# A transformer block with attention maxima folded into the scores: where the maxima are turned, and how eight PSUM banks are shared

## The chip, the cores and the metric

One NeuronCore of a Trainium2 chip runs the whole kernel. The metric is the device time of one execution in microseconds (us), as the median of several. The engines are PE (TensorE matmul, with its weight loads shown apart as PEld), DVE (VectorE), ACT (ScalarE), POOL (GpSimd) and SP (SyncE, which here only issues DMAs).

## The reference

A block of a diffusion transformer over a batch of 16 sequences of 256 tokens and 512 channels, with 16 heads of 32 channels:

```python
xn = adaln(x, cond, ln1);  q, k, v = split(xn @ qkv_w.T)
x = x + attn(rope(q), rope(k), v) @ sa_out_w.T            # layer 0: self attention
xn = adaln(x, cond, ln2)
q = rope(xn @ q_w.T); k = rope(ctx @ k_w.T); v = ctx @ v_w.T
x = x + attn(q, k, v) @ ca_out_w.T                        # layer 1: cross attention
xn = adaln(x, cond, ln3)
x = x + gelu(xn @ ffn_w1.T + ffn_b1) @ ffn_w2.T + ffn_b2
```

`adaln` normalizes each token and scales and shifts it by vectors made from the condition. All is in float32.

## The kernel before, in words

Two stages follow one another: attention, with both layers interleaved (0 to about 1450 us), and the feed-forward part (from there to the end). The change touches only the attention stage.

**Precision.** Each float32 operand is split in a high part, rounded to the type that TensorE multiplies fast, and a low rest. A product is three matmuls (high by high, high by low, low by high). The loops at lines 505 (k and q) and 501 (v and o) do so for projections; the score product has its parts stacked along the contraction, in 96 rows of `qT` and `kT`.

**Softmax.** Scores are computed twice. "scores" (line 515) puts queries on the partitions, and DVE takes the negated maximum of each row (line 739). "weigh" (line 535) computes the transposed scores with 8 more contraction rows, by which the maxima are subtracted inside the matmul; ACT takes the exponential (line 635), POOL adds the two halves of the keys (line 795), and "mix" (lines 548 and 555) multiplies by the values and sums. For the 8 rows, DVE splits the maxima of 4 heads in two parts ("max_split": a cast on line 747 and a difference on line 749), PE transposes them ("max_turn", line 524), and ACT copies them into `qT` ("max_copy", line 627). The first weigh of those 4 heads waits for the copy.

**Order.** There are 32 items (16 batch entries by two layers), each with 16 heads, that is 512 heads. A group G is 8 heads and has two halves of 4. `stage_order` writes one order of steps, and each engine runs its own steps in just this order. A place is a third of a head: scores of head n stand at place 3n, and weigh of head n - 8 at place 3n + 1. Everything else is put at places with `put`: within item i, with p = 48 i, the steps for item i + 2 (its norm, its turned x, its projections). A step of group G half h stands at 24 G + 12 h plus an offset. At equal places the order is that of the `put` calls.

**PSUM.** There are eight banks: `NS` banks used in turn by scores, weigh and max_turn (`score_users`), `NB` banks used in turn by projections, the turned x and the modulation (`bank_users`), and one for mix. A step waits on PE until the user of its bank NS (or NB) turns earlier has been read: a score by line 739, a weigh by the exponential, a max_turn by its copy; a k or q projection by the two rope products on DVE (lines 714 and 718), v by an ACT copy (line 613), o by a DVE add (line 724), turned x by ACT (line 590).

```python
score_users = [step for step in order if step[0] in ("scores", "weigh", "max_turn")]
def scores_left(step):
    n = score_turn[step] - NS
    ...
    return {"scores": max_done, "weigh": exp_done, "max_turn": maxes_copied}[old[0]], nth[old]
```

**x.** "turn_x" (PE line 488, in two halves) transposes the normalized x, ACT scales it (line 590) and rounds it ("x_high", line 599), POOL forms the rest ("x_low", line 772), and SP loads the next item's x once the second half is turned (line 802).

Of the kernel before, what the change touches and what calls it, by code (L numbers as in the profile page):

```python
# [9 lines left out]
F32R = mybir.dt.float32r  # L10
# [14 lines left out]
def stage_order(B):  # L25

    N = 2 * B
    places = {}

    def put(place, *step):
        places.setdefault(place, []).append(step)

    def weight_rows(place, rows, gap):
        for n, row in enumerate(rows):
            if n < 4:  # L40
                put(place, "w_load", *row)
        for n, row in enumerate(rows):
            put(place + gap * (n + 1), "w_split", *row)
            if n + 4 < len(rows):
                put(place + gap * (n + 1), "w_load", *rows[n + 4])

    def layer_rows(layer, m):
        return [(layer, m, c) for c in range(KC)]

    def spread(first, count, units):  # L50

        last = {}
        for n, unit in enumerate(units):
            place = first + n * count // len(units)
            put(place, *unit)
            last[unit[:4]] = place
        return last

    def project(m, i, t):
        return [("project", m, i, t, c) for c in range(KC)]  # L60

    def turns(last):
        for step, place in last.items():
            put(place + 5, "rope_high", *step[1:])
            put(place + 7, "rope_low", *step[1:])
            put(place + 7, "spill", *step[1:])

    def shares(*stretches):

        last = {}  # L70
        for first, count, units in stretches:
            last.update(spread(first, count, units))
        return last

    for i in range(-1, N):
        p, ahead = 48 * i, i + 2
        if 0 <= i < 2:
            put(p + 24, "mod_load", i + 1, 0)
            put(p + 24, "mod_load", i + 1, 1)
            for c in range(KC):  # L80
                put(p + 44 + c, "mod", i + 1, c)
                if c + 2 < KC:
                    put(p + 44 + c, "mod_load", i + 1, c + 2)
        if ahead < N + 2:
            put(p - 13, "stats", ahead, 0)
            put(p - 5, "stats", ahead, 1)
            put(p - 4, "norm", ahead)
            put(p + 1, "scale", ahead, 0)
            put(p + 5, "scale", ahead, 1)
            x_place = p + (31 if ahead == B else 20)  # L90
            for half in range(2):
                put(x_place + 3 * half, "turn_x", ahead, half)
                put(x_place + 2 + 3 * half, "x_high", ahead, half)
                put(x_place + 4 + 3 * half, "x_low", ahead, half)
        if ahead < N:
            if ahead >= B:
                put(p - 10, "ctx_load", ahead)
                put(p + 6, "ctx_split", ahead)
            k, q, v = (project(m, ahead, 0) + project(m, ahead, 1) for m in "kqv")
            if ahead < B:  # L100
                turns(shares((p + 29, 6, k[:4]), (p + 45, 7, k[4:])))
                spread(p + 66, 11, v)
            else:
                turns(spread(p + 18, 11, k))
                if ahead == B:
                    spread(p + 45, 7, v)
                else:
                    shares((p + 29, 6, v[:4]), (p + 45, 7, v[4:]))
            turns(spread(p + 52, 14, q))
        if i >= 1:  # L110
            put(p + 20, "res_load", i - 1)

            spread(p + 36, 9, [("project", "o", i - 1, t, c) for cs in (range(KC - 1), (KC - 1,)) for t in range(T) for c in cs])
            put(p + 47, "store", i - 1)
        if i == B - 2:
            weight_rows(p + 6, layer_rows(1, "k"), 2)
            weight_rows(p + 30, layer_rows(1, "v"), 2)
            weight_rows(p + 38, layer_rows(1, "q"), 2)
        if i == B:
            weight_rows(p + 45, layer_rows(1, "o"), 2)  # L120
        if i == N - 2:
            weight_rows(p - 14, [("ffn", k % (3 * KC), 0) for k in range(KC, 4 * KC)], 4)
    for G in range(2 * N):
        for half in range(2):
            put(24 * G + 12 * half + 10, "max_split", G, half)
            put(24 * G + 12 * half + 15, "max_turn", G, half)
            put(24 * G + 12 * half + 16, "max_copy", G, half)
        if G:
            put(24 * G - 20, "stack", "k", G)
            put(24 * G - 17, "stack", "q", G)  # L130

    for quad in range(4 * N):
        place = 3 * (4 * quad + LAG + 5) + 2
        for n, kind in enumerate(("mix", "invert", "divide", "o_split", "o_low")):
            put(place + 2 * n, kind, quad)

    rows = {m: layer_rows(0, m) for m in MATS}
    for row in rows["k"]:
        yield ("w_load", *row)
    for c in range(KC):  # L140
        yield ("mod_load", 0, c)
    for t in range(T):
        yield ("stats", 0, t)
    yield ("norm", 0)
    for t in range(T):
        yield ("scale", 0, t)
    for before, after in zip(rows["k"], rows["q"]):
        yield ("w_split", *before)
        yield ("w_load", *after)
    for c in range(KC):  # L150
        yield ("mod", 0, c)
    for half in range(2):
        yield ("turn_x", 0, half)
    for half in range(2):
        yield ("x_high", 0, half)
        yield ("x_low", 0, half)
    for before, after in zip(rows["q"], rows["v"]):
        yield ("w_split", *before)
        yield ("w_load", *after)
    yield from project("k", 0, 0)  # L160
    yield from project("k", 0, 1)
    for before, after in zip(rows["v"], rows["o"]):
        yield ("w_split", *before)
        yield ("w_load", *after)
    for m, after in ("kq", "qv"):
        for t in range(T):
            yield ("rope_high", m, 0, t)
            yield ("rope_low", m, 0, t)
            yield ("spill", m, 0, t)
            if t == 0:  # L170
                yield ("stack", m, 0)
        if m == "k":
            yield ("pick",)
        for t in range(T):
            yield from project(after, 0, t)
    for row in rows["o"]:
        yield ("w_split", *row)
    for place in sorted(place for place in places if place < 0):
        yield from places.pop(place)

    HEADS = 16 * N
    for n in range(HEADS + LAG + 6):
        for part in range(3):
            if part == 0 and n < HEADS:
                yield ("scores", n)
            if part == 1 and n >= LAG and n - LAG < HEADS:
                yield ("weigh", n - LAG)
            for step in places.pop(3 * n + part, ()):
                yield step
    assert not places, places  # L190
    yield ("res_load", N - 1)
    for t in range(T):
        yield from project("o", N - 1, t)
    yield ("store", N - 1)


def block_kernel(nc, x, condT, ctxT, lnT, lnb, attnT, w1T, b1, w2T, b2, cos, sin, pick, ident_in, x1, x2, out):
# [63 lines left out]
        elif (step[0] == "project" and step[4] == 0) or (step[0] == "mod" and step[2] == 0):  # L261
            bank_users.append(step)
    bank_turn = {step: n for n, step in enumerate(bank_users)}
    NB = 4

    score_users = [step for step in order if step[0] in ("scores", "weigh", "max_turn")]
    score_turn = {step: n for n, step in enumerate(score_users)}
    NS = 3

    with ExitStack() as whole:  # L270

# [31 lines left out]
        with ExitStack() as stage:  # L303
# [349 lines left out]
            def attention_vector(eng):  # L653
                eng.memset(neg_half[:, :], -0.5).then_inc(constants_set, 1)
                eng.memset(max_parts[:, :, 0:ROWS], 0.0).then_inc(parts_cleared, 1)
                for step in order:
# [84 lines left out]
                    elif kind == "max_split":  # L741
                        G, half = step[1:]
                        eng.wait_ge(max_done, HG * G + OH * (half + 1))
                        if nth[step] > 1:
                            eng.wait_ge(max_turned, nth[step] - 1)
                        mine = neg_max[G % 2][:, :, OH * half:OH * (half + 1)]
                        eng.tensor_copy(max_parts[:, :, ROWS:ROWS + OH].bitcast(F32R), mine).then_inc(max_hi_done, 1)
                        eng.wait_ge(max_hi_done, nth[step])
                        eng.tensor_tensor(max_parts[:, :, ROWS + OH:MROWS], mine, max_parts[:, :, ROWS:ROWS + OH],
                                          ALU.subtract).then_inc(max_split, 1)  # L750
                    elif kind == "divide":
                        quad = step[1]
                        eng.wait_ge(den_inverted, quad + 1)
                        eng.tensor_tensor(o_sb[:, :], ps_o[:, 0, 0:L], o_sb[:, :], ALU.mult).then_inc(o_divided, 1)
# [459 lines left out]
```

## Time and profile before

| | us |
|---|---|
| median of 3 runs | 2187.68 (2186.64 to 2192.2) |
| the profiled execution | 2184.93 |
| its span in the trace | 2183.1 |
| PE busy in the span | 2051.2 (94%) |
| DVE, ACT, POOL busy | 1111.4, 1029.1, 860.9 |
| mean granted clock of TensorE, as a share of full speed | 0.978 |

A row of a group of instructions gives line, engine, operation, output and inputs with shapes, count, busy time, mean ns of one, and how long the engine sat idle before them with the releaser. A row of the chain of waits gives who waited for whom, us in total, number of times, longest. A row of the timeline gives start, duration, engine, line, operation, count, and in brackets the idle time before it. Matmuls are pipelined and their ends are modelled: two rows that follow each other without a gap overlap by some 0.16 us.

### The profile page before, as it was taken

To read this page: it belongs to the slowest core of one execution; us is meant where nothing else is said; L and a number is where in the kernel's file an instruction comes from. 1 tells how busy PE (TensorE), PEld (TensorE's weight loads), DVE (VectorE), ACT (ScalarE), POOL (GpSimd) and SP (SyncE) were. 2 spreads that over 40 slices of the span, in tenths; PEclk is the share of its full clock that TensorE was granted. 3 is DMA by queue.
4 is the path that set the end of the run, shared out by engine and by line. 5 is a ranking of instruction groups with operands and counts; after the bars stand their busy time and mean duration, and the time that the engine had idled before them with its cause. 6 is when DMAs were issued, how large, how long until landed. Compare 5 with 4: busy or idle time off the path is not lost. (4 is left out here: it accounts for less than half of the span.)

```text
span 2183.1 us, 37400 instructions
## 1 busy us (share of the span) xinstructions
PE 2051.2 (94%) x13632; PEld 1687.3 (77%) x13632; DVE 1111.4 (51%) x1940; ACT 1029.1 (47%) x1858; POOL 860.9 (39%) x946
## 2 busy tenths in 40 slices
PE   6799999999998899999999998789999999999999
PEld 6688777777777678878878887568888888888887
DVE  4554766766676667767666666633222221222221
ACT  2344555555555656656656655644232332323322
POOL 1344555555555566666666665530101100011010
PEclk9888999999999999999999999899999999999999
DMA  5655656656556677576676676631101101011010
GB/s 180 178 154 145 174 160 168 166 155 174 160 156 173 174 198 204 160 208 175 170 198 179 175 202 172 153 121 48 58 20 39 58 1 58 20 39 58 1 39 20
DMA packets 239346, 277.93 MB, mean 127 GB/s; under 512 B 13888, under 2 KB 194368, under 8 KB 239168
## 3 DMA queue, kind: packets, MB, share of 16 engines
q1 hardware_dynamic: 239168, 275.55, 45.5%
q8 instruction: 112, 1.84, 0.4%
q14 instruction: 66, 0.54, 0.1%
HBM read 183.23 MB, written 92.27 MB: 126 GB/s over the span
## 5 line engine op out<-in xcount | busy, mean ns | idle before, releaser
L795 POOL TENSOR_TENSOR sums_sb<-prob 128x256 f32<-128x256 f32 x512 | 381.0, 749 | 392.9 <-ACT prob L635 391.1
L739 DVE TENSOR_REDUCE neg_max<-ps_s 128x2 f32<-128x512 f32 x512 | 346.4, 686 | 363.0 <-PE ps_s L515 360.7
L635 ACT ACTIVATE prob<-ps_s 128x512 f32<-128x512 f32 x512 | 305.7, 597 | 464.4 <-PE ps_s L535 462.0
L1093 DVE TENSOR_TENSOR h_lo<-h_sb,h_hi 128x512 fp32r<-128x512 f32 x128 | 92.2, 721 | 515.2 <-ACT h_hi L1054 515.2
L1050 ACT ACTIVATE h_sb<-ps_h,b_sb 128x512 f32<-128x512 f32 x128 | 88.1, 688 | 490.7 <-PE ps_h L993 490.7
L789 POOL TENSOR_TENSOR rope_c<-rope_c,rope_s 128x512 f32<-128x512 f32 x128 | 175.6, 1372 | 143.3 <-DVE rope_s L718 142.2
L515 PE MATMUL ps_s<-kT,qT 96*128 96x256 f32 x1024 | 224.1, 300 | 8.0 <-DVE neg_max L739 5.7
L535 PE MATMUL ps_s<-qT,kT 104*128 104x256 f32 x1024 | 221.0, 298 | 7.8 <-DVE neg_max L739 6.1
L515 PEld LDWEIGHTS ps_s<-kT,qT 96*128 96x128 f32 x1024 | 167.3, 192 | 72.7 <-issue 52.1
L505 PE MATMUL ps_g<-xx_hi,w_hi 128*128 128x256 f32 x1024 | 213.1, 290 | 5.5 <-POOL xx_lo L772 3.1
L505 PE MATMUL ps_g<-xx_hi,w_lo 128*128 128x256 f32 x1024 | 210.0, 287 | 0.0
L505 PE MATMUL ps_g<-xx_lo,w_hi 128*128 128x256 f32 x1024 | 209.6, 287 | 0.0
L1107 POOL TENSOR_TENSOR f_res<-f_res,b_sb 128x512 f32<-128x512 f32 x32 | 44.1, 1407 | 389.8 <-DMA f_res<-x_after_cross 389.8
L535 PEld LDWEIGHTS ps_s<-qT,kT 104*128 104x128 f32 x1024 | 170.9, 194 | 25.5 <-DVE neg_max L739 8.4
L505 PEld LDWEIGHTS ps_g<-xx_hi,w_hi 128*128 128x128 f32 x1024 | 163.3, 195 | 7.0 <-POOL xx_lo L772 3.5
L505 PEld LDWEIGHTS ps_g<-xx_lo,w_hi 128*128 128x128 f32 x1024 | 162.6, 195 | 0.0
L505 PEld LDWEIGHTS ps_g<-xx_hi,w_lo 128*128 128x128 f32 x1024 | 162.0, 194 | 0.0
L548 PE MATMUL ps_o<-prob,v_sb 128*32 128x256 f32 x2048 | 141.1, 394 | 2.5 <-ACT prob L635 2.5
L627 ACT ACTIVATE qT<-ps_s 8x1024 fp32r<-8x1024 f32 x128 | 130.3, 1018 | 3.1
L524 PE MATMUL ps_s<-ident,max_parts 128*104 128x128 f32 x256 | 54.8, 297 | 75.5 <-DVE neg_max L739 70.0
L772 POOL TENSOR_TENSOR xx_lo<-xT,xx_hi 128x512 fp32r<-128x512 f32 x68 | 101.5, 1493 | 31.6 <-ACT xx_hi L599 31.6
L731 DVE TENSOR_TENSOR rot_lo<-rope_c,rot_hi 128x512 fp32r<-128x512 f32 x128 | 107.1, 837 | 8.3 <-ACT rot_hi L620 8.1
(114 smaller groups left out, 4453.1 us busy)
## 6 DMA issues: line engine op xcount, KB each, us to landing
kT<-k_turned SPq DMA_DIRECT2D x192, 256.0 KB, 5.3
qT<-q_turned SPq DMA_DIRECT2D x64, 512.0 KB, 6.9
k_turned<-rot_hi SPq DMA_DIRECT2D x64, 256.0 KB, 4.6
k_turned<-rot_lo SPq DMA_DIRECT2D x64, 256.0 KB, 4.6
q_turned<-rot_hi SPq DMA_DIRECT2D x64, 256.0 KB, 2.4
q_turned<-rot_lo SPq DMA_DIRECT2D x64, 256.0 KB, 2.5
qT<-q_turned SPq DMA_DIRECT2D x64, 256.0 KB, 7.8
xn<-in_x SPq DMA_DIRECT2D x16, 512.0 KB, 4.9
```

What stands on the lines that cost most here:

```text
L505: ins = eng.matmul(ps_g[:, b, s * L:(s + 1) * L], w[:, row, (T * s + t) * P:(T * s + t + 1) * P], a[:, c, :], start=c == 0 and j == 0 and ...
L515: ins = eng.matmul(ps_s[:, score_bank(step), t * L:(t + 1) * L], qT[0:ROWS, G % NG, j, t * P:(t + 1) * P], kT[0:ROWS, G % NG, j, :], start ...
L535: ins = eng.matmul(ps_s[:, score_bank(step), t * L:(t + 1) * L], kT[:, G % NG, j, t * P:(t + 1) * P], qT[:, G % NG, j, :], start=True, sto ...
L548: ins = eng.matmul(ps_o[j * HD:(j + 1) * HD, 0, 0:L], v_sb[i % NV][:, k, c * P + j * HD:c * P + (j + 1) * HD], prob[:, (OH * quad + j) % N ...
L627: eng.activation(qT[ROWS:MROWS, G % NG, OH * half:OH * (half + 1), :], ps_s[ROWS:MROWS, score_bank(step), 0:L].unsqueeze(1).broadcast_to([ ...
L635: eng.activation(prob[:, n % NP, :, :].rearrange("p t l -> p (t l)"), ps_s[:, score_bank(step), :], ACT.Exp, scale=HD ** -0.5).then_inc(ex ...
L731: eng.tensor_tensor(rot_lo[:, n % NT, :, :], rope_c[n % 2][:, :, :], rot_hi[:, n % NT, :, :].bitcast(F32), ALU.subtract).then_inc(rot_lo_d ...
L739: eng.tensor_reduce(neg_max[G % 2][:, :, j], ps_s[:, score_bank(step), :].rearrange("p (t l) -> p t l", l=L), AX.X, ALU.max, negate=True). ...
L772: eng.tensor_tensor(lo[:, ks, :], xT[:, ks, :], hi[:, ks, :].bitcast(F32), ALU.subtract).then_inc(x_low_done, 1)
L789: eng.tensor_tensor(rope_c[n % 2][:, :, :], rope_c[n % 2][:, :, :], rope_s[:, :, :], ALU.add).then_inc(rope_added, 1)
L795: eng.tensor_tensor(sums_sb[:, n % NP, :], prob[:, n % NP, 0, :], prob[:, n % NP, 1, :], ALU.add).then_inc(halves_added, 1)
L1093: eng.tensor_tensor(h_lo[a % NH][:, :], h_sb[a % 2][:, :], h_hi[a % NH][:, :].bitcast(F32), ALU.subtract).then_inc(h_lo_done, 1)
```

## The change

The transposition of the maxima is put four places later, and the copy with it. The turned x of an item is put four places earlier (16 instead of 20; the item that begins layer 1 keeps its 31), so that its first half comes ahead of the values' projection of the item before. Scores get four banks and projections three. The cast of the maxima to the rounded type is written as a maximum over an axis of one element, with the same input and output.

```diff
-            x_place = p + (31 if ahead == B else 20)
+            x_place = p + (31 if ahead == B else 16)
...
             put(24 * G + 12 * half + 10, "max_split", G, half)
-            put(24 * G + 12 * half + 15, "max_turn", G, half)
-            put(24 * G + 12 * half + 16, "max_copy", G, half)
+            put(24 * G + 12 * half + 19, "max_turn", G, half)
+            put(24 * G + 12 * half + 20, "max_copy", G, half)
...
-    NB = 4
+    NB = 3
...
-    NS = 3
+    NS = 4
...
-                        eng.tensor_copy(max_parts[:, :, ROWS:ROWS + OH].bitcast(F32R), mine).then_inc(max_hi_done, 1)
+                        eng.tensor_reduce(max_parts[:, :, ROWS:ROWS + OH].bitcast(F32R), mine.unsqueeze(3), AX.X,
+                                          ALU.max).then_inc(max_hi_done, 1)
```

## Rows read from the trace of the kernel before

**Rows 1.** The page: PE over the span; then busy us by engine, 800 to 1340.

```profile
PE 2051.2 (94%) x13632; PEld 1687.3 (77%) x13632; DVE 1111.4 (51%) x1940; ACT 1029.1 (47%) x1858; POOL 860.9 (39%) x946
...
800.00:1340.00 540.00, 522.79 (x4269) 434.67 (x4268) 371.98 (x661) 334.04 (x623) 356.76 (x388) 1.00 0.68 185
```

**Rows 2.** Chain of waits, PE and its weight loads, 80 to 680 us.

```profile
PE ps_s L524 <- DVE neg_max L739: 33.7, 27, 1.5
...
PEld ps_s L524 <- DVE neg_max L739: 46.0, 38, 1.7
```

**Rows 3.** Chain of waits, PE, 680 to 800 us.

```profile
PE ps_s L524 <- DVE neg_max L739: 11.8, 5, 5.4
PE ps_s L535 <- DVE neg_max L739: 3.8, 2, 3.1
```

**Rows 4.** Chain of waits, PE and its weight loads, 800 to 1340 us.

```profile
PE ps_s L524 <- DVE neg_max L739: 17.2, 26, 1.2
...
PEld ps_s L524 <- DVE neg_max L739: 24.9, 40, 1.4
```

**Rows 5.** Chain of waits, PE, 1340 to 1470 us.

```profile
PE ps_s L524 <- DVE neg_max L739: 7.3, 5, 3.6
PE ps_s L515 <- DVE neg_max L739: 4.8, 1, 4.8
```

**Rows 6.** Timeline of PE: a max_turn that waited, and one that did not.

```profile
439.26 0.40 PE L515 MATMUL ps_s<-kT,qT 96*128 96x256 f32 x2
441.15 0.43 PE L524 MATMUL ps_s<-ident,max_parts 128*104 128x128 f32 x2 [1.50 <-DVE neg_max L739]
...
443.89 0.50 PE L515 MATMUL ps_s<-kT,qT 96*128 96x256 f32 x2
...
451.92 0.39 PE L501 MATMUL ps_g<-w_hi,xx_lo 128*128 128x512 f32 x1
452.15 0.38 PE L524 MATMUL ps_s<-ident,max_parts 128*104 128x128 f32 x2
```

**Rows 7.** Timeline of DVE, then POOL, in the same microseconds.

```profile
438.61 1.21 DVE L747 CAST max_parts<-neg_max 128x8 fp32r<-128x8 f32 x1
439.85 0.64 DVE L749 TENSOR_TENSOR max_parts<-neg_max,max_parts 128x8 f32<-128x8 f32 x1
440.42 1.28 DVE L739 TENSOR_REDUCE neg_max<-ps_s 128x2 f32<-128x512 f32 x2
...
438.50 1.29 POOL L789 TENSOR_TENSOR rope_c<-rope_c,rope_s 128x512 f32<-128x512 f32 x1 [2.17 <-DVE rope_s L718]
```

**Rows 8.** Lines 747 and 749: ns least/median/greatest, first and last start.

```profile
L747 DVE CAST max_parts<-neg_max x128: 154/684/1223, 85.0 to 1432.4; 128x8 fp32r<-128x8 f32 x128
...
L749 DVE TENSOR_TENSOR max_parts<-neg_max,max_parts x128: 166/168/662, 85.2 to 1432.8; 128x8 f32<-128x8 f32 x128
```

**Rows 9.** Timeline in layer 1: end of a q projection, the following weigh, the rope.

```profile
1119.33 0.40 PE L505 MATMUL ps_g<-xx_lo,w_hi 128*128 128x256 f32 x2
...
1122.15 0.40 PE L535 MATMUL ps_s<-qT,kT 104*128 104x256 f32 x2
...
1120.37 0.68 DVE L718 TENSOR_TENSOR rope_s<-ps_g,sin_sb 128x512 f32<-128x512 f32 x1
```

**Rows 10.** The copy (page); timeline of ACT and PE ahead of a half's first weigh.

```profile
L627 ACT ACTIVATE qT<-ps_s 8x1024 fp32r<-8x1024 f32 x128 | 130.3, 1018 | 3.1
...
1135.03 0.62 ACT L620 ACTIVATE rot_hi<-rope_c 128x512 fp32r<-128x512 f32 x1
...
1136.40 0.40 PE L535 MATMUL ps_s<-qT,kT 104*128 104x256 f32 x2
```

**Rows 11.** Start-up: DVE reads the first q projection; a wait of PE.

```profile
48.36 0.68 DVE L718 TENSOR_TENSOR rope_s<-ps_g,sin_sb 128x512 f32<-128x512 f32 x1
...
PE ps_g L488 <- DVE xn L678: 14.1, 1, 14.1
```

**Rows 12.** Timeline of DVE and PE where layer 1 begins.

```profile
728.44 0.69 DVE L663 BATCH_NORM_STATS2 stats<-xn 128x6 f32<-128x512 f32 x1 [3.89 <-DMA xn<-x_after_self]
...
729.78 0.67 PE L524 MATMUL ps_s<-ident,max_parts 128*104 128x128 f32 x2 [5.37 <-DVE neg_max L739]
```

## The prediction

> **What bounds the kernel now.** I read the page of the profile first: PE is busy 94% of the span, and in a steady stretch of layer 1 for 522.79 of 540 us, with DVE at 372, ACT at 334 and POOL at 357 [rows 1]. So PE sets the time, and the only time to be had without fewer matmuls is what PE sits idle. The chain of waits, asked for PE alone in four stretches, says where: nearly all of it stands before line 524, max_turn, and is ended by the maximum on DVE [rows 2 to 5]. The four rows of line 524 make 33.7 + 11.8 + 17.2 + 7.3 = 70.0 us, in 63 waits.
>
> Who is late is seen in one wait. max_turn starts at 441.15, after 1.50 us idle [rows 6]. On DVE the cast and the difference of the maxima are through at 440.49, but PE waits longer, until the first of the two maxima that start at 440.42 ends, at 440.42 + 0.69 = 441.11 [rows 7]. That is the score two heads back: with three banks, max_turn takes the bank of that score. So the wait is one for a bank, behind a DVE queue that the split itself makes long: cast 1.21 and difference 0.64, where the shortest of each are 0.154 and 0.166 us [rows 8]. The cast started 0.11 us after POOL's rope addition (438.50 to 439.79) and ended 0.03 after it [rows 7].
>
> **How large the stall is.** The printed 1.50 understates it, since the end of the matmul before is modelled. From start to start the waiting max_turn comes 1.89 us after its predecessor, and the one that did not wait 0.23 us [rows 6]: the stall is 1.66, 0.16 more than printed. With 0.16 for each printed wait, 80 to 680 us holds 33.7 + 27 x 0.16 = 38.0; the weight loads, which see small stalls too, say 46.0 [rows 2]. I take 42. 800 to 1340 us: 17.2 + 26 x 0.16 = 21.4 against 24.9 [rows 4], I take 23. 680 to 800: 11.8 + 3.8 + 7 x 0.16 = 17 [rows 3]. After 1340: 7.3 + 4.8 + 6 x 0.16 = 13 [rows 5], of which line 524 has 8.
>
> **The change, part by part.**
>
> *max_turn four places later, with four score banks.* In the new order its bank was last used by the score three places after the one that it waits for now, and PE comes to it after one more pair of scores and two weighs. The order around a half is then: score, weigh, projection, mix, score, weigh, max_turn. In the case of rows 6 the new max_turn stands behind the score at 443.89, while both maxima end by 440.42 + 1.28 = 441.70 [rows 7]: 2 us to spare, and 0.5 still if the stall of 1.66 is taken off. The wait could pass to the next step that needs the late maximum. With four banks that is the score now at 443.89. Without the stall (1.66) and the two transposes (0.13) PE comes there at 442.10, 0.99 us after 441.11. So in the steady stretches nothing is late in its place, and the 42 and the 23 go.
>
> *The cast as a maximum.* The trace has no such small maximum in SBUF. Bounds: 0.154 us, the shortest cast [rows 8], and 0.69, a maximum over 512 elements from PSUM [rows 7]. I take 0.17, by the neighbours of the same 8 elements [rows 8]. On the path it is worth nothing once max_turn stands later, as DVE has the margin above; it widens that margin. By how much, the trace bounds: the pair now ends at 440.49 and began at 438.61. If neither instruction is held up, it ends at 438.95; if the difference is held up in the cast's place until POOL's addition ends at 439.79 [rows 7], at 439.96, so the margin of 0.99 grows by 0.5 to 1.5 us. Here a rule speaks against this part. The Trainium skill, SBUF — State Buffer, on the shared port pair, says that DVE in a two-port mode, or with two inputs from SBUF against a GpSimd operation that reads SBUF, locks out GpSimd and is locked out by it. By that rule the new first instruction is free and the old second one is not, so most of the wait moves from line 747 to line 749; the trace agrees so far as line 749 has durations of up to 662 ns. I take the small gain, 0.5.
>
> *The copy four places later.* The copy takes 1.02 us [rows 10] and the first weigh of the half waits for it. It moves behind one more exponential and the two ACT steps that invert a denominator, in layer 1 also behind a rotation's high part in one half of four. There ACT is through at 1135.03 + 0.62 = 1135.65, but instructions overlap by 0.1, so the copy would run from 1135.55 to 1136.57, and the weigh that needs it comes at 1136.40, or 1136.53 with max_turn (0.13) now ahead of it [rows 10]. That leaves a new wait of 0.04 plus the signal: I take 0.15, bounded by 0 and by a whole copy, 1.02. It is one half in four: about 13 items between 800 and 1340, 2 us. In the other halves no rotation stands ahead of the copy, or the weigh comes later, so I cost them at nothing; the cover is 0.5 us or so, and thin.
>
> *Three banks for projections.* The tightest new pairing in steady running is the second half of the turned x, which takes the bank of the second q projection. That ends on PE at 1119.73, its rope is read out by 1120.37 + 0.68 = 1121.05, and the new turn_x stands just behind the weigh that starts at 1122.15, that is at 1122.39 [rows 9]: 1.3 us to spare, some 0.9 when PE arrives a stall earlier and DVE does not quite follow. Cost 0, bounded by one rope's length (1.3 us) in each of 30 items, 40 us. At start-up the second v projection now waits for the first q rope, out at 49.04; that may be a few us, but PE then idles 14.1 us for the normalized x anyway [rows 11], so 0.
>
> *turn_x four places earlier.* It issues the same 8 transposes. On ACT its scaling comes ahead of an exponential of an earlier head; on POOL x_low comes earlier by the same; on SP the next x load is issued about 3.5 us earlier and passes ahead of a q spill, which has more than ten places until it is stacked. Nothing on PE waits for these. 0.
>
> *Where layer 1 begins (680 to 800).* DVE is held there by a DMA (3.89 us before the statistics, then max_turn idle 5.37) [rows 12] and by weight splits. These stay: the item that begins the layer keeps its place. PE now can go on until the score three places later, which in the steady case is 443.89 - 441.15 - 0.13 = 2.6 us of work [rows 6]. So the long waits, 5.37 [rows 12], 3.1 and another that must be about 4 in the rest of the 11.8 [rows 3], shrink by about 2.5 each, or 7.5, and of the 4 us of short ones nearly all goes: 11 of 17.
>
> *The last heads (after 1340).* There are fewer projections between scores, so the copy's margin is gone: the new waits there I put at up to 1 us in each of the last 8 halves, 5 us in all; the old 13 shrink by 10. Net 5, bounded by -5 and 13.
>
> **The sum.** 42 + (23 - 2) + 11 + 5 = 79 us. The profiled execution took 2184.93, so 2106; the median shown is 2.75 above it. Predicted median 2187.7 - 79 = 2109 us, 3.6% less. The bounds of the terms: at the least 38 + (21 - 2) + 6 - 5 = 58, with 6 where layer 1 begins; at the most 46 + 25 + 17 + 13 = 101. That is 2130 and 2087. The upper bounds of the copy (1.02 us in about 30 halves) and of the third bank (40 us) come on top of these and are the first rival's.
>
> **The rivals.**
>
> 1. *The stall goes, but part of it comes back on a thinner margin*: the copy late at more than one half in four, or the turned x at its bank. Each costs 0.5 to 1 us, in 30 to 60 places, 30 us: 2139. For it: margins of 0.04, 0.5 and 0.9 us as worked out above, and that without its stalls PE runs ahead of ACT and DVE. Against: DVE and ACT have a third of their time free [rows 1]. Chance 0.17.
>
> 2. *It comes out slower: the copy is late at every half.* Place: the first weigh of each half, waiting for line 627. Price: 128 halves; it turns the sign when the mean wait exceeds 79/128 = 0.62 us, that is when copies come about 1.2 us later than reckoned, for instance because ACT stands in front of them waiting for a rope sum from POOL. With a mean wait of 0.8: 2109 + 102 = 2211. Against: ACT is busy 334 of 540 us [rows 1], and so has the time to catch up between two halves. Chance 0.05.
>
> 3. *The change does not remove the wait, as another step takes it over at once*, the pair of scores behind it. That would need the maximum 1 us later than in rows 7. Then about a third of each stall goes, by the places gained: 2160 to 2185. The part within 0.3% of now has a chance of 0.03, the rest 0.03.
>
> A change of under 0.3%, some 6 us, could not be told from none here.
>
> **How the numbers follow.** The forecast as worked out has 0.72, and its time is the prediction. Rivals 1 to 3 have 0.17, 0.05 and 0.06. The range goes from 2092, near the most that the terms allow, to 2148, which takes in rival 1; about 0.13 is left above it and 0.05 below. Faster by over 0.3%: 0.72 + 0.17 + 0.03 = 0.92; within: 0.03; slower: 0.05.
>
> **What would show it.** In the profile of the changed kernel PE's wait at line 524 for line 739 should be under 10 us in all instead of 70, with nothing of it between 200 and 660 or 800 and 1340. An item of layer 0 should take some 3 us less (42 us over the 14 items between 80 and 680 us). Line 747 should read about 170 ns throughout, and line 749 a median well above its 168 [rows 8] if it takes over the hold-up. A new row, line 535 waiting for ACT's copy (line 627), should hold 2 to 8 us; if it holds more than 30, rival 1 or 2 is at work. A wait of line 488 for line 718 tells that three banks are too few. A wait of line 515 for line 739 of more than 20 us would be rival 3. The forecast is wrong if PE's idle time falls and the span does not.

## The result, and the profile after

The changed kernel takes 2099.64 us (median of 4 runs, 2094.36 to 2100.82) against 2188.91 us before: a ratio of 0.9586, with a 95% interval of 0.9565 to 0.9608, so 4.1% less. The forecast was 2109, with a range of 2092 to 2148. The profiled execution has a span of 2098.8 us, 84.3 less than before.

The page of the changed kernel, its first line; then the chain of waits of PE over the whole span, the longest first, against [rows 2 to 5]:

```profile
PE 2034.9 (97%) x13632; PEld 1686.8 (80%) x13632; DVE 1076.0 (51%) x1940; ACT 1037.9 (49%) x1858; POOL 864.0 (41%) x946
...
PE ps_g L477 <- DMA prob<-in_lnT: 12.9, 1, 12.9
PE ps_g L488 <- DVE xn L678: 10.4, 1, 10.4
PE ps_s L535 <- ACT qT L627: 9.8, 6, 3.0
PE ps_g L505 <- issue: 5.5, 2, 3.1
PE ps_g L501 <- DVE rope_s L718: 4.5, 2, 2.7
PE ps_s L535 <- DVE neg_max L739: 3.5, 3, 1.4
PE ps_s L515 <- DVE neg_max L739: 2.8, 2, 2.6
```

The 70.0 us of line 524 are gone from the list, all of them. What is left stands at the two ends, and for a few microseconds at the change of layers. The windows of the changed kernel (length, then busy us of PE, PEld, DVE, ACT and POOL with their instructions, the granted clock, the DMA share and GB/s) show a PE that is busy for 459.43 of 460 us in layer 1, where [rows 1] had 522.79 of 540:

```profile
780.00:1240.00 460.00, 459.43 (x3774) 383.53 (x3775) 312.92 (x582) 294.57 (x542) 310.34 (x342) 1.00 0.66 189
80.00:640.00 560.00, 556.90 (x4486) 475.79 (x4486) 376.58 (x691) 327.61 (x599) 323.81 (x367) 0.97 0.64 180
640.00:780.00 140.00, 131.95 (x1047) 109.57 (x1046) 97.60 (x171) 88.92 (x165) 87.72 (x94) 0.98 0.72 203
1240.00:1366.00 126.00, 111.15 (x886) 84.92 (x884) 77.50 (x144) 81.84 (x156) 76.38 (x90) 0.95 0.56 153
```

The timeline of PE at a max_turn of the changed kernel, to be held against [rows 6]. From start to start it follows by 0.23 us, the spacing of the one that did not wait:

```profile
404.60 0.39 PE L501 MATMUL ps_g<-w_hi,o_lo 128*128 128x512 f32 x1
404.83 0.38 PE L524 MATMUL ps_s<-ident,max_parts 128*104 128x128 f32 x2
404.96 0.48 PE L515 MATMUL ps_s<-kT,qT 96*128 96x256 f32 x2
```

The two instructions of the split, against [rows 8] (the new cast is on line 747, the difference now on line 750):

```profile
L747 DVE TENSOR_REDUCE max_parts<-neg_max x128: 143/150/160, 88.3 to 1347.1; 128x8 fp32r<-128x8 f32 x128
...
L750 DVE TENSOR_TENSOR max_parts<-neg_max,max_parts x128: 166/496/1056, 88.5 to 1347.3; 128x8 f32<-128x8 f32 x128
```

The first is never held up, at most 160 ns where the cast went to 1223. The second has taken over: its median went from 168 to 496 ns.

Whom they wait for can be counted in the same traces. In the kernel before, 71 of the 128 casts and 44 of the 128 differences took over 300 ns, and every one of these 115 ended within 0.06 us of the end of an addition on POOL (line 789 or 795). In the changed kernel the same holds for all 73 differences over 300 ns, while 71 of the 128 new first instructions ran wholly inside a POOL instruction and took no longer for it. No run moved POOL's work, so this is a coincidence in time, though one without an exception. By the rule of the Trainium skill (SBUF — State Buffer, the shared port pair) a DVE instruction with two inputs from SBUF is blocked while a GpSimd operation that reads SBUF holds the pair; the trace agrees, with the 73 of 73.

**Where the time came from.** Each item has one small DVE instruction on line 674, in its norm, which stands two items ahead (that of item 18 stands where item 16 begins, the first of layer 1). The differences of its start between two traces say how far ahead a kernel is there, and their differences what each stretch gave. In the kernel before, the stretches end at 107, 679, 782 and 1308 us. The last column but one takes the rest, up to the end of the span. Worked out from the timelines, us gained against the kernel before, rounded so that each row adds up:

| kernel | up to item 3 | 3 to 16 | 16 to 18 (layers change) | 18 to 31 | after 31 | in all |
|---|---|---|---|---|---|---|
| changed | -0.9 | 42.0 | 8.6 | 18.8 | 15.8 | 84.3 |
| a_place | 1.6 | -12.3 | 1.3 | -23.8 | -6.5 | -39.7 |
| a_banks | -0.6 | -7.0 | -2.7 | -9.6 | 5.8 | -14.1 |
| a_cast | -2.0 | 21.0 | -0.2 | 11.6 | 5.2 | 35.6 |
| a_x | -2.5 | 1.8 | -2.4 | -7.3 | 0.7 | -9.7 |
| b_no_place | 0.2 | 24.1 | 0.4 | 17.2 | 8.0 | 49.9 |
| b_no_banks | 1.5 | 14.3 | 0.2 | -0.8 | -4.6 | 10.6 |
| b_no_cast | 2.5 | 41.8 | 10.6 | 19.6 | 12.9 | 87.4 |
| b_no_x | 0.8 | 9.5 | 10.3 | 3.6 | 15.7 | 39.9 |
| c_at17 | 0.6 | 41.6 | 5.2 | 23.6 | 14.2 | 85.2 |
| c_at21 | -0.2 | -4.0 | 7.8 | -7.7 | 0.4 | -3.7 |
| c_ends | 2.3 | 41.9 | 11.5 | 18.8 | 14.9 | 89.4 |
| d_mix | 1.3 | 41.9 | 9.1 | 22.1 | 12.1 | 86.5 |

These come from one execution each. The first column scatters by some 3 us among kernels with the same steps there, so no more should be read from it.

### The profile page after: what moved, and what is told of

It reads as the page before. It is cut to its first block and busy times, and to the rows that moved or that the text cites. A ratio compares the mean times of both kernels' runs of the same rounds, so it can differ in the third digit from the quotient of the medians.

```text
span 2098.8 us, 37400 instructions
## 1 busy us (share of the span) xinstructions
PE 2034.9 (97%) x13632; PEld 1686.8 (80%) x13632; DVE 1076.0 (51%) x1940; ACT 1037.9 (49%) x1858; POOL 864.0 (41%) x946
## 5 line engine op out<-in xcount | busy, mean ns | idle before, releaser
L796 POOL TENSOR_TENSOR sums_sb<-prob 128x256 f32<-128x256 f32 x512 | 403.4, 793 | 337.2 <-ACT prob L635 335.7
L535 PE MATMUL ps_s<-qT,kT 104*128 104x256 f32 x1024 | 210.3, 288 | 14.6 <-ACT qT L627 9.8
L620 ACT ACTIVATE rot_hi<-rope_c 128x512 fp32r<-128x512 f32 x128 | 80.5, 629 | 64.6 <-POOL rope_c L790 59.1
L501 PE MATMUL ps_g<-w_hi,xx_hi 128*128 128x512 f32 x256 | 105.5, 412 | 4.5 <-DVE rope_s L718 4.5
```

What stands on the lines that cost most here:

```text
L501: ins = eng.matmul(ps_g[:, b, :], a[:, c, t * P:(t + 1) * P], w[:, row, :], start=c == 0 and j == 0, stop=c == KC - 1 and j == 2)
L535: ins = eng.matmul(ps_s[:, score_bank(step), t * L:(t + 1) * L], kT[:, G % NG, j, t * P:(t + 1) * P], qT[:, G % NG, j, :], start=True, sto ...
L796: eng.tensor_tensor(sums_sb[:, n % NP, :], prob[:, n % NP, 0, :], prob[:, n % NP, 1, :], ALU.add).then_inc(halves_added, 1)
```

## The experiments

Twelve kernels were run. Medians, and ratios to the kernel before with their 95% intervals:

| kernel | us | ratio |
|---|---|---|
| a_place: the later place alone | 2222.98 | 1.0156 (1.0138 to 1.0173) |
| a_banks: the banks alone | 2197.0 | 1.004 (1.0026 to 1.0054) |
| a_cast: the cast alone | 2150.03 | 0.9826 (0.9809 to 0.9842) |
| a_x: the earlier x alone | 2194.44 | 1.0031 (1.002 to 1.0041) |
| b_no_place: changed, place undone | 2136.77 | 0.976 (0.9744 to 0.9777) |
| b_no_banks: changed, banks undone | 2174.55 | 0.9926 (0.9904 to 0.9949) |
| b_no_cast: changed, cast undone | 2097.9 | 0.9587 (0.9567 to 0.9607) |
| b_no_x: changed, x undone | 2144.39 | 0.9796 (0.978 to 0.9813) |
| c_at17: max_turn at 17 | 2099.91 | 0.96 (0.9585 to 0.9615) |
| c_at21: max_turn at 21 | 2187.32 | 0.9994 (0.9981 to 1.0006) |
| c_ends: three edits at the ends | 2097.78 | 0.9588 (0.9573 to 0.9602) |
| d_mix: 17 in layer 1, 19 elsewhere | 2097.15 | 0.9576 (0.9563 to 0.9589) |

The four parts alone give +35, +9, -38 and +6 us, together +12. All at once they give -89. So no part's worth can be told without the others.

### a_place: the later place alone

```diff
-            put(24 * G + 12 * half + 15, "max_turn", G, half)
-            put(24 * G + 12 * half + 16, "max_copy", G, half)
+            put(24 * G + 12 * half + 19, "max_turn", G, half)
+            put(24 * G + 12 * half + 20, "max_copy", G, half)
```

> The kernel before, with max_turn and its copy four places later and nothing else. Theory (the wait is for a PSUM bank, and both the later place and a fourth score bank are needed): with three banks the weigh that stood behind max_turn now takes the bank of that same score, so the stall of 1.66 us moves from line 524 to line 535 and stays; line 524 waits under 5 us, line 535 for line 739 some 50 to 70; time 2175 to 2190 us. Rival (the later place alone is enough): 2105 to 2130 us, and line 535 waits no more than before.

Measured: 2222.98 us, slower than both forecasts. The chain of waits of PE:

```profile
PE ps_s L535 <- DVE neg_max L739: 52.2, 52, 3.8
PE ps_s L515 <- ACT qT L627: 40.1, 36, 3.5
```

The first row is the theory's: the wait went from line 524 to the weigh behind the old place, at nearly its old size (52.2 us), since with three banks that weigh takes the bank of the very same score. The second row was in neither forecast. With three banks the score pair that comes three turns behind max_turn takes max_turn's own bank, which is free only when ACT has made the copy. At the old place the step three turns behind was a weigh, and in the changed kernel, with four banks, it is the first weigh of the half, which needs the copy anyway. A bank that steps use in turn has two waits to it: the one of the step that takes it, and the one of the step that takes it next.

### a_banks: the banks alone

```diff
-    NB = 4
+    NB = 3
-    NS = 3
+    NS = 4
```

> The kernel before, with four banks for scores and three for projections and nothing else. Theory: max_turn then takes a bank that is long free and waits only for the split itself, which ends 0.6 us ahead of the maximum in the traced case; about 2.1 us go in each item of layer 0 (14) and 1.1 in each of layer 1 (13), some 45 us, less about 4 us at start-up, where a values' projection waits for a rope: 2140 us, 2128 to 2155; the releaser of line 524 becomes line 749. Rival (banks do not matter, the maxima are just late): 2185 to 2195.

Measured: 2197.0 us, so the expected gain of 45 us did not come. The chain of waits of PE:

```profile
PE ps_s L524 <- DVE max_parts L749: 34.9, 34, 4.2
PE ps_s L535 <- DVE neg_max L739: 20.4, 20, 6.3
PE ps_g L505 <- DVE rope_s L718: 14.2, 15, 0.9
PE ps_g L488 <- ACT v_sb L613: 11.2, 14, 0.8
```

The releaser of line 524 is now line 749, the split, as foretold: the bank is no longer what it waits for. But it still waits, for the split, half as long as before (34.9 against 70.0). And the wait for the bank has in part passed on: with four banks the weigh just behind the old place takes the bank of the late score, and line 535 waits 20.4 us where the kernel before had 6.1. On top of both, three projection banks cost 14.2 + 11.2 us that the kernel before had not. I had taken these as free, from an order in which x was already moved.

### a_cast: the cast alone

```diff
-                        eng.tensor_copy(max_parts[:, :, ROWS:ROWS + OH].bitcast(F32R), mine).then_inc(max_hi_done, 1)
+                        eng.tensor_reduce(max_parts[:, :, ROWS:ROWS + OH].bitcast(F32R), mine.unsqueeze(3), AX.X,
+                                          ALU.max).then_inc(max_hi_done, 1)
```

> The kernel before, with the cast of the maxima as a maximum over one element and nothing else. Theory: the first instruction of the pair is never held up (150 us x 128 in the changed kernel's trace read 150 ns each), but line 750 takes over the hold-up, so the maximum behind it comes only 0.5 us earlier, in some 50 stalls: 25 us, 2165 (2155 to 2180). Rival A (neither is held up once the cast is gone): each stall shrinks by up to 1.5 us, 2110 to 2135. Rival B (nothing): 2189.

Measured: 2150.03 us, 38 less, just beyond the theory's 2155 and far from either rival. The wait of PE, and the two instructions:

```profile
PE ps_s L524 <- DVE neg_max L739: 35.5, 50, 3.8
...
L747 DVE TENSOR_REDUCE max_parts<-neg_max x128: 141/151/161, 87.0 to 1397.0; 128x8 fp32r<-128x8 f32 x128
...
L750 DVE TENSOR_TENSOR max_parts<-neg_max,max_parts x128: 166/498/1029, 87.2 to 1397.1; 128x8 f32<-128x8 f32 x128
```

The wait halved, 70.0 to 35.5. On average the first instruction of the pair went from 618 to 151 ns and the second from 333 to 521: 0.47 us saved, 0.19 us taken back. What is left, 0.28 us, makes 36 us over 128 pairs, near the 38 measured. In the stretches the gain is 1.6 us for an item of layer 0 (21.0 / 13), where there are two long stalls and one short.

### a_x: the earlier x alone

```diff
-            x_place = p + (31 if ahead == B else 20)
+            x_place = p + (31 if ahead == B else 16)
```

> The kernel before, with x turned four places earlier and nothing else. Theory: nothing on PE waits for it, no change within 6 us of the kernel before (2183 to 2195). Rival: the DMA at the layer's start or POOL's order shifts the stalls, a loss or gain of over 10 us.

Measured: 2194.44 us, a ratio of 1.0031: a small loss, at the edge of the expected band. In the table it stands in layer 1 (-7.3), and in the chain of waits of PE at the old stall, which has 79 waits instead of 63:

```profile
PE ps_s L524 <- DVE neg_max L739: 76.2, 79, 4.2
```

Why the maxima come later with x turned earlier was not looked into. Nothing was gained by this part where there are four banks for projections.

### b_no_place, b_no_banks, b_no_cast, b_no_x: the change without one part

Each is the changed kernel with the hunk of its part turned back, as in the four diffs above with plus and minus exchanged.

> The changed kernel with max_turn and its copy at their old place. Theory: four banks let max_turn wait for the split alone, and the split is 0.5 us earlier by the new cast, so only 0.3 to 0.6 us stay of the stalls of 1.66 in layer 0 and about 0.1 in layer 1; the late copies of the last heads go too: 2105 to 2120. Rival (the place carries the gain): 2150 or more.

Measured: 2136.77 us, between the two. The split is waited for again, and the late score's bank too. The rows of PE over the span, then of the weight loads from 100 to 680 us:

```profile
PE ps_s L524 <- DVE max_parts L750: 19.5, 23, 4.5
PE ps_s L535 <- DVE neg_max L739: 9.0, 8, 5.1
...
PEld ps_s L524 <- ACT prob L635: 11.0, 15, 3.8
PEld ps_s L535 <- DVE neg_max L739: 10.1, 28, 1.0
```

The later place is worth 37 us, in layer 0 above all (24.1 against 42.0). There the weight loads show two small waits of about the same sum: at line 524, in the same number as PE's waits for the split, and at the weigh behind it, which takes the bank of the late score. The forecast took the stalls that stay at 0.6 us and less; they are 0.85 on average (19.5 / 23), 1.0 with the 0.16.

> The changed kernel with three score banks and four for projections. Theory: the stall stands at line 535 behind the same maximum, shorter by 0.5 us through the new cast: 2145 to 2170, and no wait of line 501 for line 718 at start-up. Rival (the later place is enough): 2095 to 2110.

Measured: 2174.55 us, 75 more than with the banks, and beyond the theory too:

```profile
PE ps_s L515 <- ACT qT L627: 30.0, 36, 3.4
PE ps_s L535 <- DVE neg_max L739: 27.1, 38, 3.9
```

The second row is what the theory had, shortened by the cast (52.2 to 27.1). The first is the wait for max_turn's own bank, as in a_place. This expectation left it out, although a_place had run before. The fourth score bank takes away both.

> The changed kernel with the old cast. Theory: with place and banks changed nothing on PE waits for the pair any more in the steady stretches, so 2100 plus at most 8 us. Rival (the cast carries a part of its own): 2115 to 2130.

Measured: 2097.9 us: no difference to the changed kernel. What is worth 38 us alone is worth nothing beside the other parts, because PE hardly waits behind the pair any more (0.6 us at line 524). The theory holds.

> The changed kernel with x turned at its old place. Theory, weak: with three projection banks the order q, v, x, v, x puts the values' second half on the bank of the second q, which has been free for long, and x on banks of k or v that are also free; 2100 within 8 us. Rival (the turned x must come first, as three banks would else be short in the steady stretches): 0.5 to 1 us for each of 30 items, 2115 to 2130, with waits at line 488 or 501.

Measured: 2144.39 us, 45 more. The theory, called weak, was wrong, and the rival's price too low:

```profile
PE ps_g L488 <- ACT v_sb L613: 29.7, 14, 2.1
PE ps_g L505 <- DVE rope_s L718: 14.2, 15, 0.9
```

With three banks and x at its old place the second half of the turned x takes the bank of the values that have just been projected, and PE waits 2.1 us for ACT in each of 14 items; in layer 1 the second half of the k projection waits 0.9 us for the rope of the first in each of 15. The two rows make 43.9 us as printed and 48.5 with 0.16 for each wait; the measured loss lies between.

### c_at17 and c_at21: other places for max_turn

```diff
-            put(24 * G + 12 * half + 19, "max_turn", G, half)
-            put(24 * G + 12 * half + 20, "max_copy", G, half)
+            put(24 * G + 12 * half + 17, "max_turn", G, half)
+            put(24 * G + 12 * half + 18, "max_copy", G, half)
```

and the same with 21 and 22.

> The changed kernel with max_turn two places earlier (17, its copy at 18). Theory (19 stands between two limits, the maximum of its bank's score on one side and the copy's margin on the other): at 17 the bank is the one of the score two heads back again, so short waits of line 524 for line 739 come back, 0.1 to 0.4 us in half of the halves, 10 to 20 us, while the copies of the last heads are in time and give back 5: 2100 to 2115. Rival (only the fourth bank matters, any place from 17 on is the same): 2092 to 2098.

Measured: 2099.91 us, the same as at 19, at the low edge of the theory. The short waits did not come back in the steady stretches. Waits of 3.6 us in two came back in the last heads, and two long ones at the change of layers (the chain of waits of PE from 650 to 760 us):

```profile
PE ps_s L524 <- DVE neg_max L739: 9.1, 2, 5.8
```

In exchange layer 1 gains 23.6 us instead of 18.8. The likely reason is in the weight loads of the changed kernel from 770 to 1240 us, a row that is gone in c_at17:

```profile
PEld ps_s L535 <- ACT qT L627: 5.2, 12, 0.4
```

> The changed kernel with max_turn two places later (21, its copy at 22). Theory: the copy's margin of 0 to 1 us at three halves in four is used up by the 1.6 us; line 535 waits for line 627 about 1 us in one half in four and 0.2 to 0.5 in two more, 30 to 60 us in all: 2125 to 2160. Rival (the margin is larger than reckoned, the copy only counts in the last heads): 2100 to 2112.

Measured: 2187.32 us. Two places more cost 88 us, the whole gain, and the theory's 2125 to 2160 is far off:

```profile
PE ps_s L535 <- ACT qT L627: 73.3, 97, 5.0
```

Ninety-seven of the 128 halves now wait for their copy, 0.76 us each, or 0.92 with the 0.16 that a printed wait leaves out: 89 us. The margins were as thin as said, and 30 to 60 us was too little: I had let one half in four wait by 1 us and two more by 0.2 to 0.5.

### c_ends: the waits at the ends

```diff
+    put(-24, "pick")
     for G in range(2 * N):
+        late = 17 if G >= 2 * N - 4 else 19
...
-            put(p - 13, "stats", ahead, 0)
+            put(p - (8 if ahead == B + 1 else 13), "stats", ahead, 0)
```

with `late` in place of 19, and the old place of "pick" taken out.

> The changed kernel with three edits where it still waits: the constant rows of kT written later on DVE (they stand ahead of the first q rope, for which the values' projection waits 2.65 us), the first statistics of the item behind the one that begins layer 1 five places later (DVE stands 4.69 us for a DMA there), and max_turn at 17 in the last four groups. Theory (each of these waits is real time): the first maximum 3 us earlier, 3 to 5 us less at the change of layers, and 5 to 8 less in the last heads: 2088 (2080 to 2094). Rival (these waits only shift to the next step): 2096 to 2103.

Measured: 2097.78 us, a ratio of 0.9588 beside the changed kernel's 0.9586: no gain that these runs can show, where the theory had 2080 to 2094. The rival holds. In the last heads the wait for the copy went, and others stood up (PE from 1250 to 1380 us):

```profile
PE ps_s L524 <- DVE neg_max L739: 4.7, 3, 3.2
PE ps_s L535 <- ACT prob L635: 3.2, 3, 1.9
PE ps_o L548 <- ACT prob L635: 3.0, 2, 1.7
```

### d_mix: the better place for each layer

```diff
     for G in range(2 * N):
+        late = 17 if 2 * B + 4 <= G < 4 * B - 4 else 19
```

with `late` in place of 19, and the statistics as in c_ends.

> The changed kernel with max_turn at 17 in layer 1 (groups 36 to 59) and at 19 elsewhere, and the first statistics of the item behind the one that begins layer 1 five places later. Theory: place 17 takes away the wait of the weight loads of line 535 for the copy (5.2 us in 12 times in the changed kernel's trace, none with 17), and keeps 19 where 17 lost 3.4 us (the change of layers) and 1.6 (the last heads): an item of layer 1 in the steady stretch 0.37 us shorter, 4 to 5 us in all, and 1 us from the statistics: 2094 (2090 to 2098), no wait of line 535 for line 627 between 800 and 1230. Rival (the waits come back elsewhere): 2098 to 2102.

Measured: 2097.15 us, inside the theory's range (2090 to 2098), less than 1 us below the rival's; ratio 0.9576 (0.9563 to 0.9589). The mechanism came as expected, 22.1 us instead of 18.8 from item 18 to 31 and no wait of weigh for the copy between 800 and 1230 us, but the last heads gave it back in this execution (12.1 instead of 15.8; weigh waits there 8.5 us for copies instead of 6.8). It is the lowest ratio measured, and its interval overlaps with the changed kernel's: not shown to be better.

## Why the prediction was right

**What bounds it.** Right. PE set the time before and after, and its stall before line 524 was the time to be had.

**The size of the stalls.** Items 3 to 16 gave 42.0 us; the term was 42. That it fits so well is partly luck. The count with 0.16 us on each printed wait gave 38.0 from 80 to 680 us and the weight loads 46.0, and 42 was taken halfway, not worked out. Over just the stretch of the items, 107 to 679 us, the two readings are 32.3 + 26 x 0.16 = 36.5 and 44.3: PE's printed waits miss 11 small stalls that the weight loads show, and the weight loads say a little too much. Of 42.0 us, the printed waits alone are 32.3.

**Layer 1, 23 less 2 for late copies.** 18.8 us over items 18 to 31, just under the least allowed (19). The term was mis-sized by its second part: one half in four it was, as reckoned, but the weight loads wait for the copy 0.43 us in each of 12 items, 5.2 us, where the prediction took 0.15, with up to a whole copy as the bound. c_at17, which has no such wait, has 23.6.

**The bank and the place.** The reading that the wait was one for a bank, and that it would pass to another step unless the fourth bank came with the later place, is shown by a_place (52.2 us at line 535) and by a_banks (line 524 released by the split). What the prediction did not see is the third wait, of a score pair for max_turn's own bank: 40.1 us in a_place. It does not arise in the change, where the step that takes this bank needs the copy anyway, so no number failed by it.

**The cast at nothing.** Right: b_no_cast is equal. Of the bounds of 0.5 and 1.5 us for the pair, the small one, by which the second instruction stays held up, was nearer: a_cast gave 38 us over some 80 stalls, counting those that [rows 2] and [rows 4] show on the weight loads only.

**turn_x earlier at nothing.** The edit does cost nothing, but the sentence hid its worth: without it three banks for projections cost 45 us (b_no_x). The margin of 1.3 us at the third bank, [rows 9], was worked out in the new order and so took it in without saying so.

**Start-up at nothing.** The two waits of line 501 for a rope came (4.5 us). In the changed kernel's trace the first items are 3.3 us late, and 0.9 by item 3, but b_no_cast has the same two waits and is 0.8 late at item 1: the cover held.

**The change of layers: 11.** 8.6 us measured. The prediction had no new wait there, but weigh now waits for the copy once, for 3.0 us of the 9.8 in the first list.

**The last heads: 5.** This is the term that was furthest off: 15.8 us, above its own upper bound of 13. The old idle time was taken from two rows, 13 us. Idle time of PE from the norm of item 31 on fell from 25.4 us (all rows of the waits from 1307 to 1451) to 14.9 (1239 to 1367), by 10.5 where I had netted 5. The new waits for the copy were 6.8, near the 5 foreseen; what was missed is that most of the other waits went too, and that the granted clock rose with them. The windows of the kernel before, then of the changed one (the third number from the right is the granted clock):

```profile
1340.00:1360.00 20.00, 15.20 (x91) 12.01 (x94) 9.58 (x19) 8.33 (x15) 5.92 (x9) 0.83 0.60 172
1360.00:1380.00 20.00, 14.52 (x124) 11.57 (x124) 14.96 (x25) 13.83 (x28) 10.44 (x11) 0.89 0.82 221
1380.00:1400.00 20.00, 15.99 (x107) 11.06 (x108) 12.34 (x25) 9.95 (x19) 10.05 (x12) 0.84 0.60 143
1400.00:1420.00 20.00, 16.54 (x123) 10.24 (x122) 9.49 (x20) 13.69 (x26) 12.04 (x16) 0.76 0.47 108
```

```profile
1280.00:1300.00 20.00, 17.14 (x154) 14.03 (x156) 18.00 (x31) 17.35 (x34) 14.37 (x16) 0.93 0.87 226
1300.00:1320.00 20.00, 18.73 (x132) 13.26 (x124) 15.44 (x29) 10.40 (x20) 11.63 (x14) 0.81 0.71 190
1320.00:1340.00 20.00, 15.65 (x116) 11.12 (x116) 10.27 (x23) 15.15 (x29) 13.02 (x18) 0.91 0.36 84
```

What is missing to 1.00, times 20 us, is 0.17 + 0.11 + 0.16 + 0.24 = 0.68, or 13.6 us, before, and 0.07 + 0.19 + 0.09 = 0.35, or 7.0 us, after. So 6.6 us of clock and 10.5 us of idle time, 17 in all, stand against 15.8 measured. With the missing share taken of PE's busy time alone, 10.7 before and 6.2 after, it is 4.5 of clock and 15.0 in all. This is an account and not a test: no run held the clock and changed the waits.

**The signs.** The wait of line 524 is gone, an item of layer 0 is 3.2 us shorter, line 747 reads 150 ns, the difference's median is well above 168, no wait of line 488 for line 718 appears, and line 515 waits 2.8 us for line 739, far from rival 3's 20. One sign was missed: line 535 waits 9.8 us for the copy, where 2 to 8 had been given; this is still far from the 30 of rivals 1 and 2.

**The rivals.** Rival 1, a thinner margin, came true in small: 5.2 us of the copy in layer 1 and 3.0 where the layers change, against its 30. Rival 3, another step taking the wait over, did not happen with all parts in place, but it is what a_place and, in part, a_banks show when one is missing. Rival 2, the late copy, was priced at 0.62 us of mean wait as the point where it turns the sign. c_at21 is that case: 73.3 us printed, 89 with the ends, and the gain is used up, with the mean over 128 halves at 0.69. The distance to it was two places, some 1.7 us of PE's time, where the prediction had put the turn of the sign at 1.2 us.

**The sum.** 79 forecast, 84.3 in the two traces and 89 in the medians. Layer 1 and the change of layers took 2.2 and 2.4 off and the start-up 0.9, the last heads put 10.8 on. The total holds because the two steady stretches, four fifths of it, were sized well (60.8 us against 63). At the start, the change of layers and the end, the misses have opposite signs, which was luck.

## What to carry to other kernels

A wait that the profile gives to an engine can be one for a buffer; ask which step last held the bank, and count in the new order both who takes it and who takes it next, before moving anything. Parts of such a change don't add up (here +12 us one by one and -89 together), so an edit that does nothing or harm alone may be what makes the others free, and one that gains 38 us alone may be left out. A step between two waits has a margin on each side: here 17 and 19 were equal and 21 lost everything.

## What the runs showed of the hardware

A DVE cast of 8 elements took from 154 to 1223 ns, and each of the 71 that took over 300 ns ended together with a POOL instruction. The same rounding written as a maximum over one element took 141 to 161 ns in 128 of 128 cases, in two kernels. The two-input difference behind it then went up to 1056 ns.

After most idle times of two microseconds and more, matmuls ran at about half the rate for a while. In the kernel before, behind an idle time of 2.14 us, the pairs follow each other by 0.43 us instead of 0.24, and the granted clock of 1370 to 1372 us reads 0.50, the lower of TensorE's two levels (1.2 instead of 2.4 GHz):

```profile
1369.02 0.67 PE L524 MATMUL ps_s<-ident,max_parts 128*104 128x128 f32 x2 [2.14 <-DVE neg_max L739]
...
1369.91 0.63 PE L505 MATMUL ps_g<-xx_hi,w_hi 128*128 128x256 f32 x2
1370.34 0.63 PE L505 MATMUL ps_g<-xx_hi,w_lo 128*128 128x256 f32 x2
```

The same reading of 0.50 stands behind the idle times of 4.20 (at 696 us), 5.37 (730), 4.80 (1349) and 3.57 us (1381). But an idle time of that size is neither enough for it nor needed. One of 3.06 us in the same trace left the clock at 1.00; and in the changed kernel it reads 0.50 from 110 to 125 us and again from 165 to 175, with PE busy throughout and no idle time of PE since 105 us. What PE had run just before the clock fell were, both times, two groups of the modulation's matmuls (line 477); whether they are the reason was not tested. The kernel before has both stretches too, so they take no part in the difference between the two. The wait of 3.06 us and the clock behind it, then the changed kernel from 110 us:

```profile
721.59 0.50 PE L535 MATMUL ps_s<-qT,kT 104*128 104x256 f32 x2 [3.06 <-DVE neg_max L739]
...
722.00:724.00 2.00, 2.00 (x11) 1.67 (x10) 1.89 (x2) 2.00 (x6) 1.72 (x2) 1.00 1.09 199
...
110.00:115.00 5.00, 5.00 (x26) 5.00 (x25) 0.17 (x1) 0.90 (x2) 0.73 (x1) 0.50 0.64 210
```

The stalls of up to 1.66 us that returned in every item did not have this effect. In layer 1 the clock reads 1.00 [rows 1], and in the rest of layer 0, where the longest of them stand, it does so too (the kernel before):

```profile
400.00:680.00 280.00, 263.32 (x2143) 217.37 (x2142) 188.32 (x325) 158.75 (x296) 155.29 (x181) 1.00 0.63 165
```
